# A decoder layer's selective scan: timetables of their own for the first two batches, and keys and values one batch later

## What is computed

```python
hidden = rmsnorm(layernorm(x), norm_w)
x, z = split(hidden @ W_in)                     # 512 -> 2 x 1024
x = silu(causal_conv(x, 4 taps) + conv_b)
x_dbl = x @ W_x                                 # 64 ranks, B (16), C (16)
dt = softplus(x_dbl[:, :64] @ W_dt + b_dt)
A = -exp(A_log)                                 # 1024 x 16
h = exp(dt * A) * h + (dt * x) * B              # for each of 224 steps
y = sum_n(h * C) + x * D
out = residual + (y * silu(z)) @ W_out
# cross-attention, later: keys = context @ Wk + bk, values = context @ Wv + bv
```

## Time and profile before

| | us |
|---|---|
| median of 3 runs (lowest to highest) | 3691.86 (3690.65 to 3693.34) |
| the profiled execution, its own time | 3686.78 |
| its span | 3685.5 |
| first scan starts | 120.18 |
| last product with C ends | 1989.38 |
| DVE busy over the span | 2669.0 (72%) |
| PE busy over the span | 3223.5 (87%) |

### The profile page before, as it was taken

One profiled execution on the slowest core, in us unless ns is written; L12 is line 12 of the kernel. 1 busy time (PEld: TensorE's weight loads), 2 busy tenths in 40 slices (PEclk: granted clock), 3 DMA queues, 4 the chain that ended last, 5 costly groups with the idle time before them and its releaser, 6 DMA issues. The chain is left out here.

```text
span 3685.5 us, 59574 instructions
## 1 busy us (share of the span) xinstructions
PE 3223.5 (87%) x20864; PEld 2263.1 (61%) x20864; DVE 2669.0 (72%) x4681; ACT 2382.6 (65%) x5276; POOL 1775.0 (48%) x1052
## 2 busy tenths in 40 slices
PE   5699889898899889898785799999999999789998
PEld 4566556665566556665543466666666666467887
DVE  3699999999999999999996566766676676422221
ACT  4777787778877787778853566666676666432222
POOL 1678787878788787878784000000000000035454
PEclk8899999999999999999998899999999999889999
DMA  4767666676567666676552231211211121111010
GB/s 124 193 164 194 178 165 156 184 189 171 145 175 194 177 167 152 186 188 173 154 131 78 83 90 46 82 50 45 69 64 45 50 82 46 33 50 46 23 46 23
DMA packets 286440, 425.14 MB, mean 115 GB/s; under 512 B 28641, under 2 KB 226273, under 8 KB 281538
## 3 DMA queue, kind: packets, MB, share of 16 engines
q1 hardware_dynamic: 273920, 410.75, 40.7%
q10 hardware_dynamic: 12226, 10.59, 1.0%
HBM read 320.25 MB, written 101.02 MB: 114 GB/s over the span
## 5 line engine op out<-in xcount | busy, mean ns | idle before, releaser
L668 POOL TENSOR_TENSOR a_hs<-a_rep,a_bmat 128x896 f32<-128x896 f32 x512 | 1062.2, 2094 | 325.3 <-PE a_yps L235 290.1
L344 ACT ACTIVATE a_states<-a_rep,a_a_neg 128x224 f32<-128x224 f32 x2048 | 795.8, 437 | 98.0 <-DVE a_hs L573 95.3
L566 DVE TENSOR_TENSOR_SCAN a_states<-a_states,a_hs 128x900 f32<-128x900 f32 x384 | 780.1, 2031 | 107.1 <-ACT a_states L344 107.1
L1179 DVE CUSTOM_DVE_ANT_0 b_sc<-b_sps,b_mask 112x375 f32<-112x375 f32 x1024 | 500.3, 545 | 144.9 <-PE b_sps L990 144.6
L1006 PEld LDWEIGHTS b_tps<-b_ident,b_sc 112*125 112x125 f32 x3072 | 400.2, 190 | 279.8 <-issue 143.3
L1272 POOL TENSOR_TENSOR b_xt<-b_xt,b_bo 112x512 f32<-112x512 f32 x32 | 40.8, 1297 | 1063.6 <-DVE b_ln L1156 1063.6
L1006 PE MATMUL b_tps<-b_ident,b_sc 112*125 112x112 f32 x3072 | 490.0, 288 | 71.2 <-ACT b_sc L1097 46.0
L257 PE MATMUL a_work<-a_hT,w_in 128*128 128x224 f32 x2048 | 448.1, 376 | 74.9 <-ACT a_hT L376 64.9
L1097 ACT ACTIVATE b_sc<-b_sc,b_nmax 112x750 f32<-112x750 f32 x512 | 468.0, 916 | 52.0 <-DVE b_nmax L1185 52.0
L257 PEld LDWEIGHTS a_work<-a_hT,w_in 128*128 128x128 f32 x2048 | 413.5, 204 | 115.4 <-ACT a_hT L376 68.6
L573 DVE TENSOR_TENSOR a_hs<-a_states,a_cmat 128x896 f32<-128x896 f32 x384 | 419.2, 1092 | 13.2
(11 more groups left out here) (143 smaller groups left out, 4910.6 us busy)
## 6 DMA issues: line engine op xcount, KB each, us to landing
a_rep<-du_scratch SPq DMA_DIRECT2D x512, 224.0 KB, 5.6
w_in<-W_in_dram SPq DMA_DIRECT2D x128, 512.0 KB, 4.6
du_scratch<-a_du SPq DMA_DIRECT2D x16, 1792.0 KB, 11.1
ctx<-ctxT_dram SPq DMA_DIRECT2D x48, 500.0 KB, 4.2
v_scratch<-kv_out SPq DMA_DIRECT2D x96, 250.0 KB
k_scratch<-kv_out SPq DMA_DIRECT2D x96, 250.0 KB, 2.9
b_keys<-k_scratch SPq DMA_DIRECT2D x16, 1500.0 KB, 11.6
b_v<-v_scratch SPq DMA_DIRECT2D x16, 1500.0 KB
```

Source lines behind the costliest of these rows:

```text
L344: e = act.activation(rows(states[:, g % DA, :])[:, q, 1:ROW], rep[tile % REPS][:, j, 0, :], ACT.Exp, scale=a_neg[:, g % SLOTS, q:q + 1])
L566: dve.tensor_tensor_scan(state if g % G4 else whole, state, whole, 0.0, ALU.mult, ALU.add).then_inc(S["scan"], 1)
L668: pool.tensor_tensor(hs[g % RING][:, :, 1:ROW], rep[tile % REPS][:, j, 1, :].unsqueeze(1).broadcast_to([P, Q, L]), bmat[b % 2][:], ALU.mul ...
L1179: dve.tensor_tensor_reduce(out=sc[block % 2][:, j, cols], in0=sps[0:TT, j, 0:HALF], in1=mask[:, block % 2, cols], scale=-1.0, scalar=3.0e3 ...
```

## The change

Four edits, all in `mamba_phase`.

1. Each batch gets its own table of slots. `FIRST` (batch 0) does the four x units one after the other, then dt, and z behind it: two z units beside dt, the other two after `store_du`. `SECOND` (batch 1) starts its row statistics 16 slots before the first scan, and does its x and z units in slots 0 to 7, one a slot, beside the scan of batch 0; dt follows in slots 12 to 15. `LATER` (from batch 2) is the table of before, but for batch b < 8 it is 8 - b slots later; from batch 8 it is what it was.
2. Keys and values: none beside the scan of batch 0; 12 units in each of batches 1 to 14 in the same slots as before; 24 units beside batch 15, in 24 of its first 30 slots. `Wk`, `Wv` and the first context pieces are loaded at slot 16, not at slot -4.
3. The waits for the weights leave the start of POOL; ACT and DVE have theirs, with the work on `a_neg` and `log_small`, behind `normalise` and the row statistics of batch 0. PE still waits for all of it before its first instruction.
4. DVE clears only the border column of each state and ring buffer, not the whole buffer.

```diff
-    KV_SLOTS = (1, 3, 5, 9, 12, 16, 18, 20, 22, 24, 26, 31)
-        n_const = 3 + DA + RING
+        n_const = 6
+        FIRST = {
+            "row_stats": [-65], "squares": [-60], "guess": [-58], "gains": [-54], "h": [-53], "hT": [-51], "keep_hT": [-50],
+            "load_x": [-67, -66, -48, -47], "load_z": [-46, -45, -26, -25], "x": spaced(-49, 1), "tap": spaced(-48, 1),
+            "older_taps": spaced(-47, 1), "z": [-30, -29, -24, -23], "keep_z": [-29, -28, -23, -22], "residual": [-19],
+            "silu_x": [-43], "x_dbl": [-42], "xd": [-41], "store_bc": [-41], "dt": spaced(-40, 1), "parts": spaced(-39, 1),
+            "series": spaced(-38, 1), "logs": spaced(-37, 1), "skip": [-32, -31], "spread": [-28], "dt_sum": [-30],
+            "silu_z": [-20], "u": [-28], "store_du": [-27]}
+        SECOND = {
+            "load": [-20], "row_stats": [-16], "squares": [-15], "guess": [-14], "gains": [-13], "h": [-12], "hT": [-11],
+            "keep_hT": [-10], "load_x": [-9, 1, 3, 5], "load_z": [-8, 2, 4, 6], "x": spaced(0, 2), "tap": spaced(1, 2),
+            "older_taps": spaced(2, 2), "z": spaced(1, 2), "keep_z": spaced(2, 2), "residual": [9], "silu_x": [9],
+            "x_dbl": [10], "xd": [11], "store_bc": [11], "dt": spaced(12, 1), "parts": spaced(13, 1),
+            "series": spaced(14, 1), "logs": spaced(15, 1), "skip": [18, 19], "spread": [17], "dt_sum": [20],
+            "silu_z": [21], "u": [21], "store_du": [22]}
+        when = [FIRST, SECOND] + [{name: [b * SLOTS + max(8 - b, 0) + at for at in slots_of] for name, slots_of in LATER.items()}
+                                  for b in range(2, B)]
+        usual = (1, 3, 5, 9, 12, 16, 18, 20, 22, 24, 26, 31)
+        dense = [at for at in range(30) if at not in (7, 10, 16, 20, 24, 28)]
+        kv_slot = [w * SLOTS + at for w in range(1, B - 1) for at in usual] + [(B - 1) * SLOTS + at for at in dense]
...
-            act.wait_ge(S["weights"], 16 * n_weights)
-            act.activation(a_neg[:], a_neg[:], ACT.Exp).then_inc(S["a_exp"], 1)
...
+                for b, _ in due(slot, "h"):
+                    normalise(b)
+                if slot == -52:
+                    act.wait_ge(S["weights"], 16 * n_weights)
+                    act.activation(a_neg[:], a_neg[:], ACT.Exp).then_inc(S["a_exp"], 1)
...
-                dve.memset(states[:, i, 0:CHUNK], 0.0).then_inc(S["const"], 1)
+                dve.memset(rows(states[:, i, :])[:, :, 0:1], 0.0).then_inc(S["const"], 1)
             for tile in hs:
-                dve.memset(tile[:], 0.0).then_inc(S["const"], 1)
+                dve.memset(tile[:, :, 0:1], 0.0)
...
-            pool.wait_ge(S["weights"], 16 * n_weights)
-            pool.wait_ge(S["const"], n_const)
```

More of the change, by code:

```diff
@@ L193, in mamba_phase, with spaced @@
         ALL = B * SLOTS
-        slots = range(-62 - EARLY, ALL + 50)
+        slots = range(-68, ALL + 50)
         n_weights = 11
-        n_const = 3 + DA + RING
+        n_const = 6
+        def spaced(first, step):
+            return [first + step * pair for pair in range(PAIRS)]
+        FIRST = {
[5 more added lines that the diff above has]
+            "silu_z": [-20], "u": [-28], "store_du": [-27]}
@@ new lines, in mamba_phase @@
+        LATER = {
+            "load": [-68], "row_stats": [-65], "squares": [-60], "guess": [-58], "gains": [-54], "h": [-53], "hT": [-51],
+            "keep_hT": [-50], "load_x": spaced(-52, 4), "load_z": spaced(-50, 4), "x": spaced(-49, 4), "tap": spaced(-48, 4),
+            "older_taps": spaced(-47, 4), "z": spaced(-47, 4), "keep_z": spaced(-46, 4), "residual": [-35], "silu_x": [-33],
+            "x_dbl": [-32], "xd": [-31], "store_bc": [-31], "dt": spaced(-30, 2), "parts": spaced(-29, 2),
+            "series": spaced(-28, 2), "logs": spaced(-26, 2), "skip": [-20, -19], "spread": [-19], "dt_sum": [-18],
+            "silu_z": [-17], "u": [-16], "store_du": [-15]}
@@ L197, in mamba_phase @@
+        kv_at = {slot: n for n, slot in enumerate(kv_slot)}
+        assert len(kv_slot) == UNITS * B
         halves = [slice(i * M // 2, (i + 1) * M // 2) for i in range(2)]
@@ L378, in keep_hT, with keep_kv @@
                     e.then_inc(S["hT"], 1)
[L380 to L382 removed]
+            def keep_kv(n):
+                out, bank = kv_out[n % OUTS], bank_of["kv", n]
                 act.wait_ge(S["kv_ps"], n + 1)
@@ L487, in scalar_program @@
                     decays(slot + 1)
[L488 to L516, removed]
@@ new lines, in scalar_program @@
+                for b, _ in due(slot, "residual"):
+                    scale_residual(b)
+                for b, _ in due(slot, "keep_hT"):
+                    keep_hT(b)
+                for b, pair in due(slot, "tap"):
+                    last_tap(b, pair)
+                for b, pair in due(slot, "keep_z"):
+                    keep_z(b, pair)
+                for b, _ in due(slot, "silu_x"):
+                    silus_x(b)
+                for b, _ in due(slot, "xd"):
+                    keep_xd(b)
@@ L517, in scalar_program @@
+                for b, pair in due(slot, "parts"):
+                    softplus_parts(b, pair)
+                for b, pair in due(slot, "logs"):
+                    softplus_log(b, pair)
+                for b, _ in due(slot, "silu_z"):
+                    silus_z(b)
+                for b, half in due(slot, "skip"):
+                    skip(b, half)
+                if slot - 1 in kv_at:
+                    keep_kv(kv_at[slot - 1])
                 if slot >= 0 and slot // every < len(pieces) and slot % every == every // 2:
```

150 lines of the change are left out of this document (74 added, 76 removed).

## The result

The changed kernel took 3720.01 us (median of 4 runs, 3712.05 to 3722.77), the kernel before, beside it, 3691.26 (4 runs, 3686.57 to 3693.34). The ratio is 1.0076, 95% interval [1.0057, 1.0095]: slower, and outside the range of 3673 to 3699. The profiled execution took 3721.62; its span is 3720.3, 34.8 us longer than that of before.

What follows compares the result with a forecast made beforehand. DVE was taken to set the pace in middle batches, with PE nearly as full. Terms -22.7 + 3.4 + 0 + 16.7 - 1 = -3.6 took the profiled 3686.8 to 3683.2, median 3688 us; range 3673 to 3699.

Steps and rivals of the forecast that it cites:

- The start: Up to the first scan: it would come at 97.5 instead of 120.18 us, -22.7 us, bounds 92 to 102.
- the last z pieces would land about 8 us behind `store_du`: At the start: z's first late piece, queued behind `store_du`, would land at 74 us, bounds 69.8 to 78.
- The activation table: At the start: a switch costs its 1.28 us load only; by the page, 2.8 us more and a gain of 19.9.
- Batch 0: First batch's scan: three more sets of taps on DVE would make it 122.8 us, +3.4, bounds -0.3 to +7.7.
- W_in's pieces: Rival for batch 0: late pieces of W_in hold ACT and the decays; 3699 at 150 GB/s; chance 3 in 20.
- Batch 15: Last batch: twelve more units make PE last, 117.2 us against 100.5, +16.7, bounds +13 to +20.
- The rival that this batch hides its keys and values: Rival for batch 15: PE's gaps absorb the added units, sum -20.3, total 3671.6 us; chance 1 in 10.
- Batches 1 to 14: Middle batches: same instructions, six batches by about 1 us either way, so 0, bounds -6 to +5.
- two meetings of the moved work: Batches 2 to 7, on ACT: a parts slot pairs with `keep_kv` (+0.7 us), or the silus part from the skips.
- The prediction's own sign of being wrong: Middle batches: the prediction is wrong if batches 1 to 7 move by more than 6 us together.
- the rest: After batch 15: PE reaches the last sum after 4 us of rest, not 6, so -1 us.

Runs made afterwards that it cites:

- kv18_silu15_z: Changed kernel with 18 keys and values units in each of the last two batches, `silus_z` at slot 15, z's last loads ahead of `store_du`: 3701.80 us.
- kv18_18: Changed kernel with 12 units of keys and values in batches 1 to 13 and 18 in each of the last two: 3701.14 us.
- after_pool: Changed kernel with `softplus_sum` or `scale_x` (and `store_du`) one slot later from batch 2 on, wherever directly ahead of POOL's product with C: 3667.65 us.
- kv_as_before: Changed kernel with 12 keys and values units beside every scan again, weights loaded at slot -4: 3714.37 us.
- before_pool: Kernel before with `scale_x` at slot 17 instead of 16 and `store_du` one slot later: 3669.55 us.
- whole_clears: Changed kernel with the eight ring buffers cleared whole again, border columns of the state buffers as changed: 3723.30 us.
- early4_pool: Kernel before with all preparing work two slots later, `softplus_sum` one slot later on POOL, `scale_x` and `store_du` two slots later: 3704.89 us.
- early3: Kernel before with the whole preparation of every batch three slots later (EARLY = 3 instead of 6): 3749.60 us.

## Why the prediction was wrong

**The start** ended as forecast (97.47 for 97.5), and so did most of its steps: PE's first transpose 13.85 (14.0), `store_du` 66.08 (65.8), z's end 83.2 (83.2), POOL's inputs begun at 91.77 (93.7 less 2). That the last z pieces would land about 8 us behind `store_du` was the choice that mattered, and kv18_silu15_z confirms it from the other side. In between, two misses cancelled, which is luck. The silu began at 35.57, 1.8 us ahead of the 37.4 forecast, because the table load ran beside the older taps and the sum had put it behind them; and from the silu to the end of u took 30.5 us for 28.3, of which `x_dbl` alone is 2.1 (5.32 us, where before has 3.24).

The activation table was as the row said. ScalarE: Activation LUTs (the Trainium skill, "What ACT_TABLE_LOAD costs") adds a drain of 1.38 us to the load. The trace doesn't agree: the load begins 0.02 us behind `keep_z`, takes 1.28, and the silu follows it by 0.02.

**Batch 0** was +2.5 for +3.4, and DVE 112.69 busy for 113.1. W_in's pieces didn't starve it. Two small misses add up to the 0.9: 0.4 us less busy and 0.5 less idle.

**Batch 15** was +16.1 for +16.7, PE busy for 113.57 of 116.9 for the 114 of the sum. The rival that this batch hides its keys and values is refuted. Weight loading was busy for 68.15 us and PE had no gap: as a measure of TensorE's headroom, which Perfetto Trace Analysis (the Trainium skill, "Identifying the Most-Contended Engine") makes of it, it would have left room that wasn't there. kv18_18 shows the same sum from below: 18 units need 18 x 3.5 + 27.3 + 3 = 93.3 (93.60 measured), no more than DVE's 93.6, and the batch is back at 100.6.

**Batches 1 to 14** is the step that failed: "The same instructions, and from batch 8 on in the same slots ... six batches by about 1 us either way: 0, bounds -6 to +5". It looked at two meetings of the moved work, both on ACT, and not at POOL, though the row of `softplus_sum`'s kind was there: 3.98 us for `scale_x`, 3.6 times a product of DVE's and nearly twice one of POOL's inputs. The term measured +37.4. What the runs showed in its place is a chain through four engines: POOL's two 4 us instructions late at a product with C, PE's sum behind it, the units behind that, ACT in `keep_kv` or `keep_z`, the next decays, DVE. It costs up to 6.3 us a batch (after less after_pool, batch 5), by the slots where the two fall. Nor were batches 8 to 14 spared, whose tables hadn't changed (+6.5). The question which instructions the moved work is moved past had to be asked of POOL's program too. The prediction's own sign of being wrong, batches 1 to 7 off by more than 6 us together, came true with +30.9.

The three causes that could have been instead are out: keys and values a batch later (kv_as_before), the low clock (before against before_pool, after against after_pool), the clears and the phase at which the scan starts (whole_clears). That the POOL order is the cause is shown by two pairs that differ in nothing but it and the store that follows, after and after_pool, before and before_pool, and by PE's waits, which fall in the batches that the tables name. early4_pool moves two instructions at once.

With that order taken out of both kernels, the sum comes out, in part by luck: from before_pool to after_pool the start is -23.8, batch 0 +3.6, batches 1 to 14 +3.2 (1633.9 to 1637.1), batch 15 +16.0, the rest -1.0. That is -2.0, against -3.6 predicted, and the medians are 3669.55 and 3667.65. But the +3.2 is +9.2 in batches 1 to 7 and -6.0 in 8 to 14, where 0 was forecast for both, and neither is explained. So without that order the change moves next to nothing in all: what it gains at the start it gives to batch 15, and nearly all of its loss is the slots of two instructions.

**What stays open.** In after, batch 4 takes 126.4, though the preparation beside it is moved by three slots and neither instruction stands in a slot of the product's; it is 123.6 in after_pool, the slowest of its middle batches. Batch 6, which the rule doesn't touch either, falls from 121.9 to 118.0. So a batch also takes over something from the one before it, and what that is wasn't found. In batch 4 DVE waits 5.6 us for PE's sum at slot 9 (3.9 in after_pool). In early3, moved by three slots too, both long instructions lie between the same two products and the second comes late all the same: PE's sum waits 4.30 in batch 6 until that product's end, and 3.3 to 4.6 in each of the other middle batches. That this is all of early3's 3.8 us a batch is argued from the trace, not tried. Nor is it settled why batches 9 and 11 of after take 121.7 and batches 8, 10 and 12 117.3 with the same tables; the alternation is gone in after_pool, so it needs POOL's order, but what starts it isn't known. Batch 1 falls from 124.7 to 119.7 with the rule and wasn't looked into further.

## What to carry to other kernels

When work is moved by some slots among in-order engines, list for each engine the longest moved instruction and the next instruction behind it that another engine waits for; here instructions of 4 us ahead of a product cost some 50 us in one kernel and 19 in the other, and the slot behind it was free. A forecast of "the same instructions, so nothing" needs the phase of every periodic event (here every fourth slot) against every moved one. And the baseline may hold the same fault: half a per cent lay in the kernel before, in one slot.

## What had not been expected of the hardware

PE's low clock went with the lengths of the batches and didn't set them: a sum took 3.22 us behind a wait and 1.75 otherwise, yet batches 8, 10 and 12 of after_pool, with 10.3 us at the low level, are 1.1 us shorter than those of after with 3.4. And the largest effect of all was a wait that the view of PE partly puts down to "issue" (5.11 us in batch 3 of after); only the end of POOL's product 0.1 us ahead of it told what it was.
